# Silu for the gates of the last two batches, the last residual additions on VectorE, and a new order of all engines' steps

## The reference

```python
x = x + attn(layernorm(x))              # q, k, v: 256 -> 128; softmax(q k^T / sqrt(128)) v; w_o: 128 -> 256
x = x + cross(layernorm(x), ctx, mask)  # relu(x W^T + b), relu(ctx W^T + b); masked softmax of their product, times ctx
x = x + ffn(layernorm(x))               # bitlinear(silu(bitlinear(x, w_gate)) * bitlinear(x, w_up), w_down)
```

## Time and profile before

| what | us |
|---|---|
| median of 3 runs (lowest 380.48, highest 382.34) | 381.44 |
| the profiled execution, its own time | 382.19 |
| its span, first to last instruction | 380.2 |
| TensorE busy | 364.1 |
| VectorE busy | 319.8 |
| ScalarE busy | 320.0 |
| POOL busy | 294.2 |

### The profile page before, as it was taken

How to read it: one execution, slowest core, us unless ns; L and a number is a source line. 1 busy time by engine, 2 the same in 40 slices (tenths; PEclk the granted TensorE clock), 3 DMA queues, 4 the chain that set the end, 5 groups by cost and what they waited for, 6 DMA issues and landing times.

```text
span 380.2 us, 7393 instructions
## 1 busy us (share of the span) xinstructions
PE 364.1 (96%) x2113; PEld 284.7 (75%) x2142; DVE 319.8 (84%) x921; ACT 320.0 (84%) x598; POOL 294.2 (77%) x425
## 2 busy tenths in 40 slices
...
GB/s 277 402 251 136 158 44 56 56 74 89 14 83 37 41 98 169 64 124 134 137 58 56 72 150 110 39 42 55 154 57 41 84 3 16 81 100 71 85 56 110
DMA packets 48167, 36.92 MB, mean 97 GB/s; under 512 B 39552, under 2 KB 41216, under 8 KB 47744
## 3 DMA queue, kind: packets, MB, share of 16 engines
...
...
## 4 chain that ended last, share of the span: by engine, by line
PE 79%; ACT 7%; DVE 5%; DMA 4%; issue 3%; POOL 1%; ACTq 0%; DVEq 0%; POOLq 0%; SPq 0%
PE b_bank L1047 9%; PE b_bank L1049 9%; PE b_bank L1048 9%; PE d_bank L1251 7%; PE a_bank L1047 6%; PE a_bank L1049 6%; PE a_bank L1048 6%; PE g_bank L1235 5%; PE u_bank L1235 5%; PE b_bank L1163 3%; PE a_bank L1093 3%; DMA a_xT_raw<-in_x_t 2%; PE e_bank L1047 1%; PE e_bank L1049 1%; PE e_bank L1048 1%
## 5 line engine op out<-in xcount | busy, mean ns | idle before, releaser
L674 POOL TENSOR_TENSOR c_work<-c_work 128x512 f32<-128x512 f32 x48 | 61.8, 1290 | 18.1 <-DVE c_work L1491 16.1
L716 POOL TENSOR_SCALAR c_work<-c_work,h_q 128x1024 f32<-128x1024 f32 x31 | 34.9, 1125 | 11.5 <-DVE h_q L1511 11.5
L1504 DVE TENSOR_REDUCE h_max<-c_work 128x1 f32<-128x1024 f32 x32 | 38.8, 1213 | 4.2 <-POOL c_work L674 3.6
L935 ACT ACTIVATE c_work<-g_bank,c_tanh_scale 128x512 f32<-128x512 f32 x52 | 36.0, 692 | 6.4 <-PE g_bank L1235 4.9
L1047 PE MATMUL b_bank<-ctx_hi,b_pT_hi 128*128 128x256 f32 x128 | 38.6, 302 | 0.0
L1491 DVE SCALAR_TENSOR_TENSOR c_work<-c_work,g_bank 128x512 f32<-128x512 f32 x52 | 35.3, 679 | 2.1 <-ACT c_work L935 1.8
L1049 PE MATMUL b_bank<-ctx_hi,b_pT_lo 128*128 128x256 f32 x128 | 36.1, 282 | 0.0
L1048 PE MATMUL b_bank<-ctx_lo,b_pT_hi 128*128 128x256 f32 x128 | 36.1, 282 | 0.0
L1251 PE MATMUL d_bank<-downT,c_half 128*128 128x256 bf16 x256 | 33.3, 273 | 1.5 <-ACT a_xT_raw L962 0.9
L945 ACT ACTIVATE c_half<-c_work 128x1024 bf16<-128x1024 f32 x28 | 29.7, 1066 | 4.1 <-POOL c_work L716 4.1
L1235 PE MATMUL g_bank<-gateT,xqT 128*128 128x512 bf16 x98 | 30.5, 381 | 1.5 <-ACT xqT L908 0.5
...
## 6 DMA issues: line engine op xcount, KB each, us to landing
...
```

The source lines that it names most:

```text
L674: pool.tensor_tensor(h[:, t % 2, half * HALF:(half + 1) * HALF], th[:, j % 2, :], up[:, j % 2, :], ALU.mult).then_inc(hs, 1)
L716: pool.tensor_scalar(h[:, t % 2, :], h[:, t % 2, :], h_q[:, t:t + 1], ROUND if n < LAST else ROUND_F16, ALU.mult, ALU.add).then_inc(h_roun ...
L935: act.activation(th[:, j % 2, :], gu_bank("g", j, n), ACT.Tanh, scale=c_tanh_scale[:, j // 2:j // 2 + 1]).then_inc(tanhs, 1)
L1504: dve.tensor_reduce(h_max[:, one], h[:, t % 2, :], AX.X, ALU.max, apply_absolute_value=True).then_inc(h_maxes, 1)
```

## The change

1. `SILU_FROM = 6`: for batch 6 too, `t` computes Silu instead of Tanh, and the eight `G` steps of that batch on VectorE are gone. `M` and the gate bank's next user wait for `tanhs` in place of `gates`. `scales` of batch 6 uses the constants of Silu (three small POOL instructions for five). Before the first Silu (`C.t0/6`) ScalarE waits until all exponentials of B are done (`b_exped`), so that the table changes once.
2. `POOL_O` is empty and `POOL_DN` holds batch 6 alone: the four `O` additions and `DN0` to `DN2` of batch 7 are VectorE instructions again; their seven moves on ScalarE and seven additions on POOL are gone.
3. All five orders are new, from the first loads on. On SP the first loads go W, ctxT part 1, bias, ctxT part 0, w_qkv, x, w_o, head mask in place of ctxT 0, w_qkv, ctxT 1, W, x.

```diff
+SILU_FROM = 6
-POOL_O = [(7, t) for t in range(4)]
+POOL_O = []
-POOL_DN = [(6, t) for t in range(4)] + [(7, t) for t in range(3)]
+POOL_DN = [(6, t) for t in range(4)]
 PE_ORDER (from the last cross-attention on)
-    B.O0/7 B.S3/7 C.u4/6 C.g4/6 B.P2/7 C.DN3/5 B.O1/7 B.P3/7 C.g5/6 B.O2/7 C.u5/6 B.O3/7 C.g6/6 C.xT0/7 C.g7/6
-    C.DN0/6 C.u6/6 C.u7/6 C.g0/7 C.DN1/6 C.u0/7 C.g1/7 C.xT1/7 C.u1/7 C.g2/7 C.g3/7 C.u2/7 C.xT2/7 C.u3/7 C.g4/7
-    C.g5/7 C.u4/7 C.xT3/7 C.u5/7 C.hT0/7 C.DN2/6 C.g6/7 C.g7/7 C.DN3/6 C.hT1/7 C.u6/7 C.u7/7 C.DN0/7 C.hT2/7
-    C.DN1/7 C.DN2/7 C.hT3/7 C.DN3/7""".split()
+    C.u6/5 C.g6/5 B.P0/7 B.S2/7 C.DN0/5 C.g7/5 B.P1/7 C.u7/5 B.O0/7 B.S3/7 B.P2/7 C.g0/6 C.g1/6 B.O1/7 C.u0/6
+    B.P3/7 C.u1/6 B.O2/7 C.g2/6 C.u2/6 B.O3/7 C.g3/6 C.g4/6 C.xT0/7 C.u3/6 C.g5/6 C.DN1/5 C.u4/6 C.u5/6 C.g6/6
+    C.g7/6 C.DN2/5 C.xT1/7 C.u6/6 C.g0/7 C.u7/6 C.g1/7 C.DN3/5 C.u0/7 C.xT2/7 C.u1/7 C.DN0/6 C.g2/7 C.g3/7
+    C.DN1/6 C.g4/7 C.u2/7 C.u3/7 C.g5/7 C.DN2/6 C.xT3/7 C.u4/7 C.u5/7 C.hT0/7 C.g6/7 C.g7/7 C.DN3/6 C.u6/7
+    C.u7/7 C.hT1/7 C.DN0/7 C.hT2/7 C.DN1/7 C.DN2/7 C.hT3/7 C.DN3/7""".split()
 ACT_ORDER (from the last exponential on)
-    B.exp2/7 B.mv0/7 C.hb0/6 C.t4/6 B.P2/7 B.exp3/7 B.mv1/7 C.norm0/7 B.P3/7 C.t5/6 B.mv2/7 C.hb1/6 C.xq0/7
+    C.u6/5 B.exp1/7 C.t6/5 B.P0/7 C.hb1/5 C.t7/5 B.P1/7 C.u7/5 C.hb2/5 B.exp2/7 B.P2/7 B.exp3/7 C.norm0/7 C.t0/6
+    C.t1/6 B.P3/7 C.xq0/7 C.hb3/5 C.t2/6 C.norm1/7 C.t3/6 C.cx0/7 C.t4/6 C.t5/6 C.hb0/6 C.xq1/7 C.norm2/7 C.t6/6
+    C.t7/6 C.cx1/7 C.hb1/6 C.xq2/7 C.t0/7 C.t1/7 C.cx2/7 C.hb2/6 C.mv0/6 C.norm3/7 C.t2/7 C.t3/7 C.hb3/6 C.mv1/6
+    C.xq3/7 C.t4/7 C.t5/7 C.cx3/7 C.mv2/6 C.ch0/7 C.t6/7 C.t7/7 C.mv3/6 C.ch1/7 C.ch2/7 C.ch3/7""".split()
 DVE_ORDER (the start, and from the last attention on)
-    W.cT0/0 A.xT0/0 A.xT1/0 W.cT1/0 W.lo/0 W.centre/0 A.bn0/0 A.bn1/0 A.ag0/0 W.split/0 A.ag1/0 A.bn0/1 A.bn1/1
+    W.lo/0 A.xT0/0 A.xT1/0 W.cT0/0 W.cT1/0 A.bn0/0 A.bn1/0 W.centre/0 W.wo0/0 A.ag0/0 A.ag1/0 A.bn0/1 A.bn1/1
+    W.split/0 W.wo1/0 A.ag0/1 A.ag1/1 W.rl/0 W.rs0/0 W.rs1/0 A.Q/0 A.K/0 A.V/0 A.S0/0 A.S1/0 A.N0/0 A.S2/0
...
+    B.S3/7 C.hm3/5 B.P2/7 C.hs3/5 B.inv3/7 C.mx0/7 C.hr3/5 B.O1/7 C.sc0/7 C.bn1/7 C.rc0/7 C.ag1/7 C.M0/6 C.M1/6
+    B.P3/7 B.O2/7 C.hm0/6 C.bn2/7 B.O3/7 C.hs0/6 C.mx1/7 C.hr0/6 C.M2/6 C.sc1/7 C.M3/6 C.ag2/7 C.rc1/7 C.hm1/6
+    C.DN1/5 C.hs1/6 C.M4/6 C.hr1/6 C.M5/6 C.mx2/7 C.hm2/6 C.DN2/5 C.hs2/6 C.sc2/7 C.bn3/7 C.hr2/6 C.rc2/7 C.M6/6
+    C.M7/6 C.DN3/5 C.ag3/7 C.hm3/6 C.hs3/6 C.hr3/6 C.G0/7 C.G1/7 C.mx3/7 C.hm0/7 C.sc3/7 C.hs0/7 C.rc3/7 C.G2/7
+    C.hr0/7 C.G3/7 C.hm1/7 C.hs1/7 C.hr1/7 C.G4/7 C.G5/7 C.hm2/7 C.hs2/7 C.hr2/7 C.G6/7 C.G7/7 C.DN0/7 C.hm3/7
+    C.hs3/7 C.hr3/7 C.DN1/7 C.hq3/7 C.DN2/7 C.ch3/7 C.DN3/7""".split()
 def g_read(j, n):
-    return (tanhs if n == LAST else gates), 2 * T * n + j + 1
+    return (tanhs if n >= SILU_FROM else gates), 2 * T * n + j + 1
 scales(half, n), after its waits
+    if n >= SILU_FROM:
+        pool.tensor_scalar(c_tanh_scale[:, pair], c_s[:, pair], w_mean[:, 0:1], 1.0, ALU.mult, ALU.mult)
+        pool.tensor_scalar(c_out_scale[:, pair], c_s[:, pair], k_down_last[:, :], 1.0, ALU.mult, ALU.mult)
+        pool.tensor_scalar(c_eps[:, pair], c_q[:, pair], k_eps_last[:, :], 1.0, ALU.mult, ALU.mult).then_inc(c_scales, 1)
+        return
 c_step on ScalarE
+    if n == SILU_FROM and j == 0:
+        act.wait_ge(b_exped, T * B)
-    act.activation(th[:, j % 2, :], gu_bank("g", j, n), ACT.Tanh, scale=c_tanh_scale[:, j // 2:j // 2 + 1]).then_inc(tanhs, 1)
+    act.activation(th[:, j % 2, :], gu_bank("g", j, n), ACT.Silu if n >= SILU_FROM else ACT.Tanh, scale=c_tanh_scale[:, j // 2:j // 2 + 1]).then_inc(tanhs, 1)
```

263 lines of the change are left out of this document (125 added, 138 removed).

## The result

| | before | after |
|---|---|---|
| median of 12 executions each | 381.67 us (380.48 to 382.77) | 383.67 us (381.69 to 385.77) |
| ratio after / before | | 1.0057, 95% interval 1.0041 to 1.0074 |
| profiled execution: time, span | 382.19, 380.2 | 384.7, 382.7 |

The new kernel is 0.57% slower. The forecast was 381.2 and no change; the time lies in its range (377.6 to 384.0), but over the bound of 0.5%. The range had been made wide for rivals that did not come about as they were told, so the time lies in it by luck.

A forecast was written before the change was run, and what follows sets the result against it. TensorE bounds the kernel as a whole, VectorE's chain its end. M0/6 at 345.5 + 15.4 + 12.8 = 373.7, + 6.2 gives span 380.0, start and middle 0: median 381.2 us, range 377.6 to 384.0.

The forecast's parts named there:

- step 1: Last attention on TensorE: 5.2 us of products move behind it, so S3/7 ends at 341.3 instead of 346.5.
- steps 2, 3: Behind S3/7: last exponential ends near 343.0, then a norm of 0.6; table load begins near 343.5.
- step 3: Batch 6's first product: norm 0.6, table load 1.28, Silu 0.69 put M0/6 at 345.5; hole on VectorE 0.3 us.
- step 4: VectorE's chain from M0/6 to the last quantisation: 15.4 to G0/7, then 12.8; hr3/7 ends at 373.7.
- step 5: From hr3/7 to the end: 6.2 us, or 6.7 if DN1's addition is on the path; end 379.9 to 380.0.
- Step 6: Seven moves removed on ScalarE and seven additions on POOL: worth nothing, as these engines aren't late at the end.
- Step 7: The start: Q/0 1.9 us late, swallowed by the old hole before VT/0; 0 to +0.2 us, taken as 0.
- Step 8: The middle: same TensorE work, stall under 1 us in 100; taken as 0, bounds 1.5 us either way.
- TensorE sets the end: Faster rival: the end follows TensorE, which loses 2.0 of its 4.1 us, middle gives 0.5; 378.9 us, chance 0.37.
- The cold start: Slower rival: stillness before Q/0 halves TensorE's clock, 2.4 us; 383.6 us; chance 0.20 together with late gates.
- Late gates of batch 6: Slower rival: exp3/7 ends after 343.0; 1.5 us backlog at S3/7 gives 382.7; chance 0.20 together with cold start.
- The switch of tables: Rival before the first Silu: ScalarE stands still 1.3 us beyond the table load; 382.5 us, chance 0.02.

The follow-up runs named there:

- e7: Kernel after with the last batch's seven residual additions back on a ScalarE move and POOL addition: 387.99 us, ratio 1.0165 to before.
- e14: Kernel after with the old lists up to batch 1's cross-attention projections, POOL changing over earlier, C.norm1/0 one step earlier: 381.24 us, ratio 0.9998 to before.
- e8: Kernel after with batch 6's gates by Tanh again and VectorE's eight G steps put back, order otherwise new: 388.46 us, ratio 1.0209 to before.
- e16: Kernel after, unchanged, run again with a second profile: 382.87 us, ratio 1.0042 to before.
- e2: Kernel before with the lists of after up to batch 1's cross-attention projections, the rest old: 384.62 us, ratio 1.0076 to before.

## Why the prediction missed, step by step

The rows of the end, as the prediction had asked for: the last matmul of S3/7 on TensorE; table load and first Silu on ScalarE; M0/6, G0/7, a wait and hr3/7 on VectorE; the last product.

```profile
343.42 0.40 PE L1055 MATMUL b_bank<-yp_hi,xp_lo 128*128 128x512 f32 x1
```
```profile
346.10 1.28 ACT L941 ACT_TABLE_LOAD   x1
347.39 0.69 ACT L941 ACTIVATE c_work<-g_bank,c_tanh_scale 128x512 f32<-128x512 f32 x1
```
```profile
348.17 0.69 DVE L1492 TENSOR_TENSOR c_work<-c_work,u_bank 128x512 f32<-128x512 f32 x1 [0.25 <-ACT c_work L941]
...
363.00 0.69 DVE L1492 TENSOR_TENSOR c_work<-c_work,u_bank 128x512 f32<-128x512 f32 x1
...
373.25 0.69 DVE L1492 TENSOR_TENSOR c_work<-c_work,u_bank 128x512 f32<-128x512 f32 x1 [0.83 <-PE b_bank L1207]
...
376.34 0.16 DVE L1517 RECIPROCAL h_q<-h_s 128x1 f32<-128x1 f32 x1
```
```profile
379.00 1.05 PE L1257 MATMUL d_bank<-downT,c_half 128*128 128x256 bf16 x8 [0.47 <-ACT c_half L919]
```

| stretch | forecast | measured |
|---|---|---|
| S3/7 ends on TensorE (step 1) | 341.3 | 343.82 |
| from there to the table load (steps 2, 3) | 2.2 | 2.28 |
| to M0/6 (step 3) | 4.2 | 4.35 |
| M0/6 to G0/7 (step 4) | 15.4 | 14.83 |
| G0/7 to the end of hr3/7 (step 4) | 12.8 | 13.50 |
| from there to the end (step 5) | 6.2 to 6.3 | 6.20 |
| S3/7 to the end | 38.6 to 38.7 | 38.9 |

**Steps 1 to 5 held.** Everything behind S3/7 came as long as summed, to 0.3 us. That is in part luck, as two terms of step 4 were off by 0.6 and 0.7 and cancel. The four row maxima of batch 6 took 4.6 where 5.2 was costed, with other steps in the gap ahead of them. And ahead of G6/7 stands a wait of 0.83, for TensorE's transposes hT1/7 (372.50): the new list has them behind u6/7 and u7/7, the old one ahead, which step 4 missed when it took this stretch over from the old run; DN3/6 ahead of them had waited another 0.67 for a transposing transfer. Step 1's shift, 5.2 by forecast, was 4.9 by TensorE's own end of S3/7 and 5.8 by VectorE's mark. S3/7 came 2.5 late, 2.2 of it by the start, and that lateness goes through to the end.

**Step 6** was right in sum and wrong in its reason. I called the removed moves and additions worth nothing. Undoing them costs 4.3 (e7): the last batch's statistics hang on the additions, so the way through ScalarE and POOL would have been on the path of the new order. Nothing of it is in the forecast's error, since the new kernel has the additions on VectorE.

**Step 7 is the one that failed.** It took 0 for the start, and the start costs 1.0 to 2.1 us. What it did follow came out well: Q/0 at 13.9 (forecast 14.8), V's transposes at 19.6 (20.5), the delay swallowed by the old hole of 2.05 us, of which 0.79 was left. But I stopped at that point, 20 us in, and took the next 40 us as unchanged, while the same lists had been written anew there on all engines. The loss begins right there: from 20 to 40 us TensorE is without work for 3.8 us where it was 1.0. Read on, the lists alone would have raised doubts: ScalarE has the split of ctx and the mask among batch 0's work, where the old list has them behind its exponentials, and SP issues x/3, for which bn0/3 and behind it V/1 wait, behind ctx/1. What looks worst in TensorE's list, one ctx projection between P2/1 and H/1 where there were two, cost nothing that the windows show (1.7 us without work from 40 to 60, 1.8 before).

**Step 8** (the middle, taken as 0) held: with the start taken off, middle and end together come to + 0.3 in the trace and to 0.9998 in e14.

**The rivals.** "TensorE sets the end" fell: 3.8 us without work in the last stretch instead of 2, and e8 moves the end by nearly each G step. The cold start was right in that a half clock can follow a wait and costs time, and wrong in its place and its condition: it came behind a wait of 1.5 us at 48 and not at Q/0, though Q/0 waited as long (1.52) and kept its clock. Its price was put at 2.4; an execution with a low stretch was longer by 1.5. Its condition, Q/0 later than 14 us, wasn't met in the trace of after (13.93), and in e16, where it was (14.12), the clock stayed at 1.00. That its sum, 383.6, is nearly the time measured is chance. Late gates of batch 6 were the path by which the loss showed, with the start as its cause and not a backlog at S3/7. The switch of tables costs its load: the Silu starts 1.29 us after the load begins here too, so the row again leaves no room for the drain that the Trainium skill adds (ScalarE: Activation LUTs, What ACT_TABLE_LOAD costs).

**Open:** which step of the new start it is, if it is one. Only whole starts were shown to matter (e2, e14), and the traces narrow it to what TensorE waits for between 20 and 40 us; the four repairs by single steps gave back less than their intervals, with a move among them that lost as much as the others gained. Also open is why executions at full clock still spread (378.7 to 381.1 in e16, 378.3 to 379.4 in before). The landing of x/3 can be a part: bn0/3 waited for it for 2.41 us in after, 1.50 in e16, 1.48 in e2, 1.23 in e8 and 1.13 in e7.
